# Centring the mLSTM values of four groups from the loaded rows on VectorE and GpSimd instead of with a matrix product

## The reference, cut to what matters

```python
def _L0_xattn_ref(q, k, v, w_igate, b_igate, w_fgate, b_fgate, ln_weight):   # k = v = ctx_1024
    ...
    hst = _mlstm_parallel(qh, kh, vh, ig, fg)          # ... Cn = C / normalizer; hst = Cn @ vh
    mean = hst.mean(axis=-1, keepdims=True)            # over the 32 features of a head
    var = hst.var(axis=-1, keepdims=True)
    hn = (hst - mean) / jnp.sqrt(var + 1e-05)
```

## Time and profile before

| | us |
|---|---|
| three runs | 481.88, 484.66, 485.70; median 484.66 |
| profiled execution, whole | 484.01 |
| its span, first to last instruction | 482.3 |
| stage B, groups 0 to 3 | about 152 to 198 |
| stage B, groups 4 to 7 | about 198 to 253 |

### The profile page before, as it was taken

One profiled execution on the slowest core, in us unless ns is written; L12 is line 12 of the kernel. 1 busy time (PEld: TensorE's weight loads), 2 busy tenths in 40 slices (PEclk: granted clock), 3 DMA queues, 4 the chain that ended last, 5 costly groups with the idle time before them and its releaser, 6 DMA issues.

```text
span 482.3 us, 14464 instructions
## 1 busy us (share of the span) xinstructions
PE 446.0 (92%) x5114; PEld 377.0 (78%) x5115; DVE 308.0 (64%) x993; ACT 301.1 (62%) x675; POOL 185.6 (38%) x209
## 2 busy tenths in 40 slices
PE   8999999999988999999889999988888999899984
PEld 7688888888877767666558999887877999899631
DVE  5578888888886578878875687433333544445246
ACT  5677877787675989978678745443435664232236
POOL 5522022208100111127556556366564666554300
PEclk9999999999998999999988999998898999999998
DMA  5342226700000061111121242122212232211186
GB/s 143 88 125 77 77 59 125 212 3 3 12 14 24 23 220 46 45 34 59 56 72 47 80 116 78 29 68 66 75 56 72 71 82 79 79 51 35 56 302 199
DMA packets 47485, 38.05 MB, mean 79 GB/s; under 512 B 5056, under 2 KB 40784, under 8 KB 47424
## 3 DMA queue, kind: packets, MB, share of 16 engines
q1 hardware_dynamic: 42672, 28.10, 21.2%
q0 software_dynamic: 4320, 8.92, 5.6%
q10 hardware_dynamic: 432, 0.20, 0.2%
HBM read 19.30 MB, written 16.34 MB: 74 GB/s over the span
## 4 chain that ended last, share of the span: by engine, by line
PE 54%; DVE 21%; ACT 10%; issue 6%; another core or an unknown queue 3%; DMA 3%; DVEq 1%; SPq 0%; ACTq 0%; POOL 0%; POOLq 0%
PE bank L1418 9%; PE bank L1332 6%; PE bank L1376 4%; PE bank L1386 3%; PE bank L1405 3%; PE bank L1407 2%; PE bank L1406 2%; DVE tkr L1541 2%; DVE negmax L1550 2%; DVE prob L1547 2%; PE bank L1056 2%; PE bank L1003 2%; PE bank L1005 2%; PE bank L1004 2%
## 5 line engine op out<-in xcount | busy, mean ns | idle before, releaser
L593 POOL DMA_INDIRECT routed<-rh,zbuf x71 | 74.1, 1043 | 60.5 <-DVE rh L1926 34.7
L1926 DVE TENSOR_SCALAR rh<-bank,zbuf 128x128 f32<-128x128 f32 x71 | 24.8, 349 | 53.2 <-PE bank L1418 20.2
L1418 PE MATMUL bank<-wdn,prob 128*128 x400 | 52.0, 285 | 1.1 <-issue 1.0
L1418 PEld LDWEIGHTS bank<-wdn,prob 128*128 128x128 f32 x400 | 49.8, 201 | 1.7 <-issue 1.4
L928 ACT ACTIVATE prob<-bank 128x512 f32<-128x512 f32 x50 | 29.3, 597 | 25.9 <-remote 12.0
L1405 PE MATMUL bank<-xT_hi,wq_hi 128*128 128x256 f32 x100 | 31.6, 316 | 9.9 <-ACT prob L928 7.4
L490 POOL DMA_INDIRECT slots<-zbuf,slot x32 | 31.7, 989 | 21.9 <-PE bank L1332 8.7
L490 POOL DMA_INDIRECT slots<-tkr,slot x32 | 31.6, 989 | 12.4 <-issue 6.7
L480 POOL TENSOR_TENSOR hlw<-hst,lnw 128x512 f32<-128x512 f32 x8 | 10.2, 1274 | 63.2 <-ACT hst L803 63.2
L913 ACT ACTIVATE prob<-bank 128x512 f32<-128x512 f32 x21 | 12.5, 597 | 31.1 <-PE bank L1376 29.1
L1332 PEld LDWEIGHTS bank<-sdn,qblk 128*128 128x128 f32 x256 | 30.1, 194 | 0.6
(11 more groups left out here) (303 smaller groups left out, 1228.6 us busy)
## 6 DMA issues: line engine op xcount, KB each, us to landing
slots<-x2T SPq DMA_DIRECT2D x8, 585.0 KB, 5.2
zbuf<-slots SPq DMA_DIRECT2D x25, 130.0 KB
tkr<-in_x SPq DMA_DIRECT2D x8, 256.0 KB, 3.1
cs<-in_ctx SPq DMA_DIRECT2D x8, 256.0 KB, 2.9
wup<-in_L_ffn_routed_up SPq DMA_DIRECT2D x1, 2048.0 KB, 8.4
zbuf<-tkr SPq DMA_DIRECT2D x8, 256.0 KB
wup<-routed SPq DMA_DIRECT2D x8, 256.0 KB, 3.7
wdn<-routed SPq DMA_DIRECT2D x8, 256.0 KB, 4.3
```

The source lines that it names most:

```text
L593: pool.indirect_dma_start(routed, bass.IndirectOffsetOnAxis(ap=xr[n][:, :].bitcast(I32)[:, DEST:DEST + 1], axis=0), yr[n % 4][:, :], None) ...
L1418: m = mm(bank[6 + a][:, 0:D], hTp[:, q, c // 2, c % 2, a, :], wdn[:, bass.ds(e * (FC * D) + c * D, D)], start=(c == 0), stop=(c == FC - 1))
L1926: tsc(yr[n % 4][:, :], bank[6 + n % 2][:, 0:D], xr[n % NX][:, GATE:GATE + 1], None, ALU.mult).then_inc(s["y_ok"], 1)
```

## The change

For groups 1 to 4 the centring product and the copy out of PSUM go away. VectorE sums each head's 32 features from `cs` (`head_sums`, 128x512 to 128x16), placed in `group_b(g)` behind `x2_out(g-2)` and ahead of `score(g, 1)`, for group g+1. GpSimd scales the sums by 1/32 and subtracts them from the rows of `cs`, writing `vals` (`values_p`): for group 1 ahead of its first `weighted`, for groups 2 to 4 behind `weighted(0)` to `weighted(2)`. Groups 0, 5, 6 and 7 keep the product. `cs` is two buffers; a load waits for the load before it, for the transposes of two groups before, and, where GpSimd reads that buffer, for GpSimd. `turn_ctx(g)` behind a group on GpSimd waits for `cT_ok` instead of `vals_ok`. Two waits of scatters count `vc_ps` anew, and one semaphore is shared to make room for the new ones.

```diff
-    cs = sb("cs", [P, GT, D])
+    cs = [sb(f"cs{n}", [P, GT, D]) for n in range(2)]
+    vsum = sb("vsum", [P, GT * NH])
+    vavg = sb("vavg", [P, GT * NH])
...
+    BY_PE = [0, 5, 6, 7]
+    BY_POOL = [1, 2, 3, 4]
...
         def context(g):
             if g > 0:
-                sp.wait_ge(s["cT_ps"], g)
-            sp.dma_start(cs[:, :, :], ctx_tok[:, g * GT:g * GT + GT, :]).then_inc(s["cs_ok"], 16)
+                sp.wait_ge(s["cs_ok"], 16 * g)
+            if g > 1:
+                sp.wait_ge(s["cT_ps"], g - 1)
+            if g - 2 in BY_POOL:
+                sp.wait_ge(s["valp_ok"], BY_POOL.index(g - 2) + 1)
+            sp.dma_start(cs[g % 2][:, :, :], ctx_tok[:, g * GT:g * GT + GT, :]).then_inc(s["cs_ok"], 16)
...
+        def values_p(g):
+            if g > 1:
+                pool.wait_ge(s["u_ps"], GT * (g - 1))
+            pool.wait_ge(s["cs_ok"], 16 * (g + 1))
+            pool.wait_ge(s["vsum_ok"], BY_POOL.index(g) + 1)
+            c3 = cs[g % 2][:, :, :].rearrange("p k (h d) -> p (k h) d", h=NH)
+            mst(pool.tensor_scalar(vavg[:, :], vsum[:, :], 1.0 / DH, None, ALU.mult))
+            pool.tensor_tensor(vals[g % 2][:, :, :, :].rearrange("p k h d -> p (k h) d")[:, :, 0:DH], c3,
+                               spread(vavg[:, :], [P, GT * NH, DH]), ALU.subtract).then_inc(s["valp_ok"], 1)
...
+        values_p(1)
         for g in range(1, 5):
             weighted(g - 1)
+            if g + 1 in BY_POOL:
+                values_p(g + 1)
...
         def values(g):
-            act.wait_ge(s["vc_ps"], g + 1)
+            act.wait_ge(s["vc_ps"], BY_PE.index(g) + 1)
...
-                values(g + 1)
+                if g + 1 in BY_PE:
+                    values(g + 1)
...
         def turn_ctx(g):
-            if g > 0:
-                pe.wait_ge(s["vals_ok"], g)
+            if g - 1 in BY_PE:
+                pe.wait_ge(s["vals_ok"], BY_PE.index(g - 1) + 1)
+            elif g > 0:
+                pe.wait_ge(s["cT_ok"], g)
...
-            if k == 0:
-                pe.wait_ge(s["vals_ok"], g + 1)
+            if k == 0 and g in BY_PE:
+                pe.wait_ge(s["vals_ok"], BY_PE.index(g) + 1)
+            if k == 0 and g in BY_POOL:
+                pe.wait_ge(s["valp_ok"], BY_POOL.index(g) + 1)
...
-            if after:
+            if g + 1 in BY_PE:
                 centred(g + 1)
...
+        def head_sums(g):
+            n = BY_POOL.index(g)
+            dve.wait_ge(s["cs_ok"], 16 * (g + 1))
+            if n > 0:
+                dve.wait_ge(s["valp_ok"], n)
+            dve.tensor_reduce(vsum[:, :], cs[g % 2][:, :, :].rearrange("p k (h d) -> p (k h) d", h=NH), AX.X, ALU.add)\
+                .then_inc(s["vsum_ok"], 1)
...
             if last:
                 x2_out(g - 2)
+            if g + 1 in BY_POOL:
+                head_sums(g + 1)
             if now:
                 score(g, 1)
```

More of the change, by code:

```diff
@@ L237, in decoder_layer @@
     y0, y1, fin = (a[:, :].rearrange("p (t d) -> p t d", d=D) for a in (wup, wdn, x2T))
-    names = """ld_tok ld_tok1 ld_wqk ld_conv ld_hank hank_ps bias_ok qzero_ok ld_attn ld_small ld_gw ld_wup ld_wdn ld_sh st_cpad cpad_ok
+    names = """ld_tok ld_tok1 ld_wqk ld_conv ld_hank hank_ps bias_ok qzero_ok ld_attn ld_small ld_gw ld_wup ld_wdn ld_sh cpad_ok
     const_p const_v wq_ok read_ok gwT_ps gw_ok vsteps xT_ps xT_ok xhi_ok xlo_ok
@@ L244, in decoder_layer @@
     vc_ps nrm_ok nsq_ok fabs_ok fexp_ok flog_ok igsteps al_ok rh_ok mrow_ok emx_ok floor_ok qblk_ok
-    vals_ok dd_ps decay_ok c_ok u_ps h_ok hsq_ok hva_ok hn_ok hln_ok hrs_ok res1_ok mv1_ok lnv1_ok
+    vals_ok vsum_ok valp_ok dd_ps decay_ok c_ok u_ps h_ok hsq_ok hva_ok hn_ok hln_ok hrs_ok res1_ok mv1_ok lnv1_ok
     rstd1_ok x2_ok bsteps x2T_ps lg_ps lg_ok lmax_ok lexp_ok tokb_ok lnd_ok fl_ps hlw_ok
@@ L248, in decoder_layer @@
     pre_ok mask_ok shu_ps sh_ok shd_ps shk_ps base_ok xr_ps xrT_ok up_ps wst_ok hT_ok y_ps y_ok passed_pool
-    passed_dve passed_act passed_pe mv2_ok lnv2_ok rstd2_ok fina_ok find_ok tot_ps st_fin st_out""".split()
+    passed_dve passed_pe mv2_ok lnv2_ok rstd2_ok fina_ok find_ok tot_ps st_fin st_out""".split()
     s = {n: sem(n) for n in names}
@@ L303, in _ @@
         sp.wait_ge(s["cpad_ok"], 3)
-        sp.dma_start(conv_pad, cpad[:, :]).then_inc(s["st_cpad"], 16)
-        sp.wait_ge(s["st_cpad"], 16)
+        sp.dma_start(conv_pad, cpad[:, :]).then_inc(s["st_pad"], 16)
+        sp.wait_ge(s["st_pad"], 16)
         sp.dma_start(hankel, bass.AP(tensor=conv_pad.tensor, offset=0, ap=[[1, S], [P, H], [1, S]])).then_inc(s["ld_hank"], 16)
@@ L380, in _ @@
         sp.wait_ge(s["toff_ok"], 4)
-        sp.wait_ge(s["st_pad"], 16 * E)
+        sp.wait_ge(s["st_pad"], 16 * (E + 1))
         for t in range(2 * MATES, SLOT_TILES):
@@ L494, in in_sixth @@
             weighted(4)
-            pool.wait_ge(s["vc_ps"], 7)
+            pool.wait_ge(s["vc_ps"], 3)
             scatter(0)
@@ L514, in in_seventh @@
             scatter(first)
-            pool.wait_ge(s["vc_ps"], g + 2)
+            pool.wait_ge(s["vc_ps"], 4)
             scatter(first + 1)
@@ L1125, in turn_ctx @@
         def turn_ctx(g):
-            if g > 0:
-                pe.wait_ge(s["vals_ok"], g)
+            if g - 1 in BY_PE:
+                pe.wait_ge(s["vals_ok"], BY_PE.index(g - 1) + 1)
+            elif g > 0:
+                pe.wait_ge(s["cT_ok"], g)
             pe.wait_ge(s["cs_ok"], 16 * (g + 1))
             for k in range(GT):
-                m = pe.transpose(c_bank(g)[:, k * P:(k + 1) * P], cs[:, k, :], ident[:, :])
+                m = pe.transpose(c_bank(g)[:, k * P:(k + 1) * P], cs[g % 2][:, k, :], ident[:, :])
             m.then_inc(s["cT_ps"], 1)
@@ L1283, in group_b @@
                 gates(g + 1)
-            if after:
+            if g + 1 in BY_PE:
                 centred(g + 1)
             if g == NG - 1:
-                pe.wait_ge(s["vals_ok"], NG)
+                pe.wait_ge(s["vals_ok"], len(BY_PE))
                 sh_up_mm(0, [1])
```

## The result

The changed kernel took 491.1 us (median of 5 runs, 488.43 to 493.12); the kernel before, measured in the same comparison, 485.7 us (median of 5 runs, 481.88 to 487.89). The ratio is 1.0115, interval 1.0071 to 1.0159: slower by 5.4 us. That is above the predicted 486.6 and above the end of the range, 489.5.

A forecast was written before the change was run, and what follows sets the result against it. The prediction took a loop of ScalarE and VectorE to bound stage B in groups 1 to 3. Its terms, -0.07 + 0 + 0.31 + 0.86 + 0.86 = +1.96 us on 484.66, gave 486.6 us, range 483.0 to 489.5.

The forecast's parts named there:

- Which engine bounds stage B, and what the removed work is worth: Stage B, groups 1 to 3: a ScalarE-VectorE loop bounds; removing TensorE's product gains 0, ScalarE's copies -0.07 us.
- that step: ScalarE, group 0: of the copy's 0.58 us, 0.07 is gained at `emx`; the other 0.51 becomes a wait.
- The sums in VectorE's holes: VectorE ahead of `logf`, groups 0 to 3: sums of 0.69 us fit holes of 0.89 to 1.84 us; cost 0.
- The hold-up: VectorE's `logf`: GpSimd's subtraction holds it up by 0, 0.31, 0.86 and 0.86 us in groups 0 to 3.
- Two terms: GpSimd's subtraction: lasts 1.27 us and begins 0.34 us behind the sums, from 0.02 handover and 0.32 scaling.
- The sum: Whole kernel: copy gain and hold-ups add to +1.96 us, giving 486.6 us from a median of 484.66.
- The range: Whole kernel time: 483.0 to 489.5 us, leaving out the far half of rival C and rival D.
- The rival D: TensorE in stage B: granted clock falls without the product, slower by over 1%, 491.7 us; chance 0.10.
- a sign of being wrong: TensorE: its granted clock leaving 1.00 between 156 and 200 us would show a falling clock instead of the forecast.

The follow-up runs named there:

- e1_later: Changed kernel with GpSimd's subtraction for groups 2 to 4 waiting for VectorE's keys, against the kernel before: 464.42 against 465.09 us, ratio 0.9992; repeats 0.9996 and 1.0015.
- the four comparisons: Changed kernel against the kernel before, measured anew four times on several chips: ratios 1.0115, 1.0026, 1.0016 and 1.0132.
- the delay alone: Kernel before with one unused VectorE reduce added behind `logf` in groups 1 to 3: 487.34 against 484.6 us, ratio 1.0034.
- the fourth comparison: Changed kernel unaltered against the kernel before, 6 and 23 runs: 490.56 against 487.24 us, ratio 1.0132.

## Why the prediction was right or wrong

**Which engine bounds stage B, and what the removed work is worth: right within what these comparisons can tell.** The product and the copy were put at 0.07 us. Left out for nothing, they brought +0.4 and -1.3 us, neither clear of no change, and ScalarE's freed time was waiting at `hst`. In the changed kernel `emx` waited 0.44 us for `mrow` in group 0, as that step had said for its 0.51.

**The sums in VectorE's holes: right.** They took 0.68 us, the hole ahead of `logf` in group 2 went from 0.89 to 0.29 us, and with the hold-up taken away (`e1_later`) the laps were those of the kernel before, 34.13 us.

**The hold-up: right in mechanism, and in size partly by luck.** Predicted 0, 0.31, 0.86 and 0.86 us; measured 0.03, 0.24, 0.80 and 0.79. Two terms were off and cancelled, which is luck. The subtraction took 1.05 us and not 1.27, and it began later: 178.13 (end of the sums) to 178.32 for the scaling is a handover of 0.19 us, not 0.02, so it began 0.53 behind the sums, not 0.34. Release 0.15 ahead of GpSimd's end was predicted as 0.14. The Trainium skill's rule in "Who interferes with whom" of "SBUF — State Buffer", that the first of the two to start holds the other for a whole instruction, agrees: 0.10 us decided for 0.80.

**The sum: its parts held, the total didn't.** It said +1.96 us. The laps show +1.85 to +2.25 in four executions, and the four comparisons +2.3 to +2.6 when weighted, but the first one, against which the prediction stands, +5.4. Of the 4.5 us between 486.6 and 491.1, 1.0 is the base: the prediction started from 484.66, the median of three runs, and the kernel before had 485.7 in the comparison. The step that failed is the last one, from the loop to the whole. "-0.07 + 0 + 0.31 + 0.86 + 0.86 = +1.96 us" takes everything outside groups 0 to 3 as unchanged. The routed stage has no term in it, and no reason is given for that; in the first profile it measured +4.1 us, and the laps of groups 4 to 6 another +1.55. The range then gave the time of 5 runs too little room.

**The rival D, a clock that falls,** had a chance of 0.10, by the missing product, in 156 to 200 us, at 1.7 us a fall. In the first profile the clock was 1.00 there and fell behind it. In the other three profiles of the changed kernel it did leave 1.00 between 180 and 192 us, which the prediction named as a sign of being wrong, but that went with 0.2 to 0.4 us in the laps, not 1.7. The falls aren't peculiar to a missing product: the kernel with the product kept had 0.57 in 184 to 188 us, the delay alone 0.50 in 196 to 200, and the later subtraction, without the product, 1.00 throughout 156 to 204 us in three executions.

**What stays open.** Of the 5.4 us, 1.85 are shown to be the hold-up. About 4.1 us of the first profiled span lie behind the first routed pair. On the 485 us chips that stage took 177.2 and 177.7 us in the profiled executions of the kernel before, 181.2, 180.8 and 181.7 in those of the changed kernel, but also 179.8 and 182.9 in those of the later subtraction, 179.5 with the delay alone and 179.9 with the product and the copy left out. So it was longer in each profiled execution of an edited kernel there, whatever the edit, while the ratios of the later subtraction to the kernel before are 0.9996 and 1.0015. On the 465 us chips it took 158.9 to 160.3 us in every variant, 159.4 in the changed kernel (the kernel before has no profile there), and there the change cost 0.5 us. So I couldn't tie a longer routed stage to the change. What lengthened it, and whether the 5.4 us, and the ratio of 1.0132 in the fourth comparison, are scatter of 5 and 6 runs or a cost that only some chips ask, is not settled.

## What to carry to other kernels

Work moved to GpSimd isn't hidden by GpSimd being idle: look at what VectorE runs at that moment, and put GpSimd's reads under VectorE's instructions with one SBUF input, as under `bn_stats` here, which took 0.88 us with the subtraction over it and 0.87 without. One more wait on GpSimd brought the laps back from 35.9 to 34.1 us. And before an engine is relieved, see if the chain of waits passes through it: 92% busy TensorE and a nearly full ScalarE were both beside the path.

## What was unexpected of the hardware

- The same kernel took 465 us in the comparisons on two chips and 485 on two others. The changed kernel's routed stage is where most of it lies (159.4 us against 180.8 and 181.7). The ratio of the same pair of kernels came out from 1.0016 to 1.0132, and on the two chips of 485 us alone as 1.0026 and 1.0132, further apart than their intervals.
- GpSimd's subtraction of 128x512 with an operand spread over 32 elements took 1.05 us, where `hlw` with an operand spread over the tiles took 1.27.
- An instruction that is held up this way shows no idle time before it; its own duration in the profile grows, from 0.29 to 1.09 us.
- The granted clock stayed at 1.00 with TensorE busy for 2.12 of 4 us (168 to 172), and fell to 0.52 in 208 to 212 behind two stretches with 3.44 and 3.46 us busy.
